# The W_d product of a decoder's first FFN as two float32r products of a split operand, and four instruction orders written anew

## The chip, the cores and the metric

The kernel runs on one core of one Trainium2 chip. The metric is the device time of one execution in microseconds (us); the smaller the better. Engines are named as in the profile: PE (TensorE matmuls), PEld (its weight loads), DVE (VectorE), ACT (ScalarE), POOL (GpSimd), SP (SyncE, which issues the DMAs).

## The reference

Input x is 16 sequences of 128 tokens with 256 features, and there is a context tensor of the same shape. Two decoder layers follow one another, each with post-norm residuals:

- layer 0: causal attention with 16 heads; a gated long convolution (per head an outer product of key and value, a causal convolution over the 128 positions, a product with the query); the first FFN;
- layer 1: a state-space mixer, a second long convolution, and a second FFN with a Hadamard transform.

The change is about the first FFN. For each token, x is normalised, scaled by 127 over its largest magnitude and rounded to an integer (`Q`). Then

```
g = Q @ sign(W_g).T      u = Q @ sign(W_u).T        (1024 columns each)
P = silu(inv * g) * (inv * u)                       (1024 columns, float32)
y = P @ sign(W_d).T                                 (256 columns)
x = norm(x + y)
```

so the last product multiplies full float32 numbers by a matrix that holds only -1, 0 and 1.

## The kernel before, in words

Everything stays in SBUF. A stage works item by item; an item is one sequence (128 tokens, one partition each), so each stage has 16 items, and the two long convolutions have 32 steps `mix(0)` to `mix(31)` each. Each stage is a Python function that returns small functions per engine (`f.down(n, k)`, `f.rstd(n)`, ...). The order in which an engine issues these calls is written out by hand in four functions, `tensor_order` (L1833), `scalar_order` (L1930), `vector_order` (L1999) and `gpsimd_order` (L2112); each engine runs its list strictly in order, and semaphores make a call wait for what it reads or overwrites. In the lists, `a` is attention, `m` the first convolution, `f` the first FFN, `x` the state-space mixer, `n` the second convolution, `g` the second FFN. Stages overlap only as far as the lists interleave them.

The first FFN (`ffn0`, L649 on) runs for item n:

- PE turns the convolution's result (L689), DVE adds x, takes the statistics and normalises (L804, L811, L819, L469), POOL computes 1/sqrt with two tiny instructions (L461, L463) and four more for the scale (L910 to L916, and L924); DVE finds the peak, the step and the integers (L831 to L855).
- PE turns Q (L698); `gate` and `up` multiply it by the signs of W_g and W_u, which are bf16, 512 columns at a time (L703).
- ACT takes the silu (L781), DVE multiplies (L863); the result `PM` is P with tokens on the partitions.
- `p_turn(n, k)` (L738) transposes half k of P, four blocks of 128x128, into a PSUM bank. For k = 1 that bank is also the one of `gate(n, 0)`.
- `keep_p(n, k)` (L788) copies that bank on ACT into `PMT`, 128x512 float32. There are two `PMT` buffers.
- `down(n, k)` (L750) makes four products of 256 columns; the eight of an item accumulate into one bank. The weights loaded into PE are blocks of P, the operand that streams through is sign(W_d), both float32.
- DVE adds x to the bank and normalises again (L871, L878, L880, L469), POOL gives 1/sqrt (L461, L463), PE turns the result for the next stage (L761), ACT keeps it (L794).

sign(W_d) is made by `sign0(2)` on ACT, in place (L524). Before the first FFN there is another piece of work that the orders place: the weights of the second FFN are loaded into staging tiles by SP (L502), once attention's last x is kept (`a.keep_x(15)`, L316, after PE's `a.x_turn(15)`, L264). ACT sums their magnitudes with `magnitude(0)` to `magnitude(2)` (L530), PE adds the sums over the partitions in `m.totals()` (L572), and its place in `tensor_order` is between two `mix` steps:

```
m.mix(16); a.x_turn(15)
m.mix(17); m.mix(18); m.mix(19); m.mix(20); m.mix(21); m.totals(); m.mix(22); ...
```

A `mix` step is three products of 512 float32 columns on PE (L594 to L596), two multiplications on POOL (L564), two on DVE (L608) and a sum on DVE (L619).

Of the kernel before, what the change touches and what calls it, by code (L numbers as in the profile page):

```python
# [9 lines left out]
BF16 = mybir.dt.bfloat16  # L10
ALU = mybir.AluOpType
# [3 lines left out]
P = 128  # L15
# [459 lines left out]
def mixer(ch, T, d, s, before, name, toep, skip, banks):  # L475
# [35 lines left out]
    def scalar(act):  # L511
# [9 lines left out]
        def sign0(k):  # L521
            dst, src = ((T["wgu0"][:, 1, :].rearrange("p (a w) -> p a w", a=2), T["wgu0_high"]), (T["wgu0"][:, 0, :], T["wgu0_low"]),
                        (T["wd0"][:, :, :], T["wd0"][:, :, :]))[k]
            nc.scalar.activation(dst, src, ACT.Sign).then_inc(s["signed"], 1)  # L524
# [123 lines left out]
def ffn0(ch, T, d, s, attended, mixed):  # L648
# [7 lines left out]
    PMT = two("pmt", [P, FC, S])  # L656
    ST, MV, VE, RS = two("st", [P, 6]), two("mv", [P, 2]), two("ve", [P, 1]), two("rs", [P, 1])
    ST3, MV3, VE3, RS3 = two("st3", [P, 6]), two("mv3", [P, 2]), two("ve3", [P, 1]), two("rs3", [P, 1])
    VA, VB, VC, RS2 = two("va", [P, 1]), two("vb", [P, 1]), two("vc", [P, 1]), two("rs2", [P, 1])
    MX, MS, SC, INV = two("mx", [P, 1]), two("ms", [P, 1], n=4), two("sc", [P, 1]), two("inv", [P, 1], n=4)  # L660
# [3 lines left out]
    X, XT, MIX, ident, identb, wgu, wd = (T[n] for n in ("X", "XT", "MIX", "ident", "identb", "wgu0", "wd0"))  # L664
# [12 lines left out]
    def tensor(pe):  # L677
# [28 lines left out]
        def gate(n, k):  # L706
# [7 lines left out]
            if k == 0:  # L714
                upto(pe, s["p1_kept"], n)
# [12 lines left out]
        def p_turn(n, k):  # L728
# [3 lines left out]
            upto(pe, s[f"p{k}_kept"], n)  # L732
# [33 lines left out]
    def scalar(act):  # L766
# [16 lines left out]
        def keep_p(n, k):  # L783
# [12 lines left out]
        return calls(keep_q=keep_q, silu=silu, keep_p=keep_p, keep_x=keep_x)  # L796

    def vector(dve):
# [67 lines left out]
        def add_down(n):  # L866
# [3 lines left out]
            dve.wait_ge(s["downed"], n + 1)  # L870
# [19 lines left out]
    def gpsimd(pool):  # L890
# [35 lines left out]
        return calls(rstd=rstd, rstd3=rstd3, rms=rms, step_back=step_back)  # L926
# [48 lines left out]
def state_space(ch, T, d, s, before):  # L975
# [345 lines left out]
    def gpsimd(pool):  # L1321
# [41 lines left out]
        def skip(n):  # L1363
# [3 lines left out]
            if n == 0:  # L1367
                pool.wait_ge(before["downed"], B)
# [962 lines left out]
```

## Time and profile before

| | us |
|---|---|
| median of 3 runs | 749.12 (746.75 to 749.25) |
| the profiled execution, its time | 746.65 |
| its span, first to last instruction | 744.0 |
| PE busy | 696.2 (94% of the span) |
| DVE busy | 610.1 (82%) |
| POOL busy | 538.3 (72%) |
| ACT busy | 412.4 (55%) |

"Busy" is the time in which at least one instruction of the engine ran. A matmul's recorded duration includes its way through the array and overlaps the next one, so what a matmul costs in a dense stretch is the distance from one start to the next, not the duration. PEclk is the granted TensorE clock as a share of full speed (1.00 is 2.4 GHz, 0.50 is 1.2 GHz).

### The profile page before, as it was taken

What the parts mean: (1) busy time and instruction counts of PE and PEld (TensorE: products, weight loads), DVE (VectorE), ACT (ScalarE), POOL (GpSimd) and SP (SyncE); (2) the same over time, 40 slices, a digit from 0 to 9 for tenths busy, and PEclk for the clock granted to TensorE, in tenths of its full rate; (3) what the DMA queues carried; (4) which work ended last, traced back from release to release, by engine and by line L of the source; (5) the groups of instructions that cost most, each with busy time, mean ns of one, the idle gap of its engine ahead of it and who ended that gap; (6) DMA issues with size and microseconds to landing.
All of it is one profiled execution on the core that took longest, in us unless ns stands there. A gap on an engine that the chain in (4) does not pass through costs nothing. (4 is left out here: it accounts for less than half of the span.)

```text
span 744.0 us, 13795 instructions
## 1 busy us (share of the span) xinstructions
PE 696.2 (94%) x4302; PEld 497.2 (67%) x4302; DVE 610.1 (82%) x1281; ACT 412.4 (55%) x660; POOL 538.3 (72%) x781
## 2 busy tenths in 40 slices
PE   6999999999989999999889989989999999999994
PEld 5788888754434677778667777755544457777783
DVE  4887888688979978665799899878999998877873
ACT  0665757710160744554598877872010348889784
POOL 2788798878857425530248668789898999999972
PEclk9999999999999999999999999999999999999997
DMA  8910000000300050000031121204000000000001
GB/s 282 365 52 2 2 2 3 1 1 0 141 29 1 0 217 1 1 2 1 29 103 72 44 71 34 80 1 131 1 0 1 0 2 1 15 16 15 9 22 44
DMA packets 12727, 33.39 MB, mean 45 GB/s; under 512 B 2672, under 2 KB 8048, under 8 KB 11376
## 3 DMA queue, kind: packets, MB, share of 16 engines
q1 hardware_dynamic: 12656, 32.52, 12.1%
q8 instruction: 36, 0.59, 0.3%
q14 instruction: 35, 0.29, 0.1%
HBM read 30.35 MB, written 2.16 MB: 44 GB/s over the span
## 5 line engine op out<-in xcount | busy, mean ns | idle before, releaser
L1053 PE MATMUL bank<-XT,win_late 128*128 128x256 f32 x320 | 81.3, 388 | 5.9 <-ACT ss_sz L1151 2.8
L564 POOL TENSOR_TENSOR m_kv<-CTXT 128x512 f32<-128x512 f32 x64 | 65.2, 1043 | 16.9 <-PE bank L596 16.9
L619 DVE TENSOR_REDUCE MIX<-m_pr 128x128 f32<-128x1024 f32 x64 | 77.0, 1210 | 0.3
L1238 DVE SCALAR_TENSOR_TENSOR ss_xc<-bank,cw_late,ss_xc 128x254 f32<-128x254 f32 x144 | 67.4, 477 | 4.9 <-ACT ss_xc L1142 1.4
L564 POOL TENSOR_TENSOR m_kv<-XT,CTXT 128x512 f32<-128x512 f32 x64 | 69.4, 1111 | 1.4 <-PE bank L596 1.1
L1053 PEld LDWEIGHTS bank<-XT,win_late 128*128 128x128 f32 x320 | 56.6, 190 | 17.6 <-DVE ss_xc L1238 5.6
L594 PE MATMUL bank<-m_kv,toep 128*128 128x512 f32 x128 | 66.1, 598 | 1.2 <-issue 1.2
L596 PE MATMUL bank<-m_kv,toep 128*128 128x512 f32 x128 | 66.3, 599 | 0.0
L595 PE MATMUL bank<-m_kv,toep 128*128 128x512 f32 x128 | 66.0, 597 | 0.0
L1530 PE MATMUL bank<-had_last,f_ht 128*128 128x256 f32 x256 | 60.2, 382 | 0.1
L750 PE MATMUL bank<-wd,f_pmt 128*128 128x256 f32 x256 | 59.7, 380 | 0.0
L461 POOL TENSOR_TENSOR f_ve<-f_mv,eps 128x1 f32<-128x1 f32 x48 | 9.4, 196 | 67.1 <-DVE f_mv L880 42.4
L1530 PEld LDWEIGHTS bank<-had_last,f_ht 128*128 128x128 f32 x256 | 47.3, 190 | 8.2 <-ACT f_ht L1593 0.9
L750 PEld LDWEIGHTS bank<-wd,f_pmt 128*128 128x128 f32 x256 | 47.3, 190 | 7.3 <-ACT f_pmt L788 0.5
L434 POOL TENSOR_TENSOR at_p<-at_p,at_mx 128x512 f32<-128x512 f32 x44 | 45.4, 1045 | 8.8 <-DVE at_mx L345 8.6
L280 ACT COPY at_pt<-bank 128x512 f32<-128x512 f32 x64 | 36.5, 590 | 20.4 <-PE bank L207 20.1
L596 PEld LDWEIGHTS bank<-m_kv,toep 128*128 128x128 f32 x128 | 24.6, 192 | 31.0 <-issue 31.0
L608 DVE TENSOR_TENSOR m_pr<-bank,XT 128x512 f32<-128x512 f32 x64 | 40.9, 682 | 5.3 <-PE bank L596 5.3
L595 PEld LDWEIGHTS bank<-m_kv,toep 128*128 128x128 f32 x128 | 24.3, 190 | 30.6 <-issue 30.6
L608 DVE TENSOR_TENSOR m_pr<-bank,CTXT 128x512 f32<-128x512 f32 x64 | 40.9, 682 | 2.6 <-PE bank L596 2.6
L160 PE MATMUL bank<-XT,at_wqk 128*128 128x128 f32 x256 | 34.6, 286 | 6.0 <-DMA at_hmask<-hmask_dram 5.6
L1142 ACT ACTIVATE ss_xc<-bank,cb_late,cw_late 128x256 f32<-128x256 f32 x48 | 26.9, 563 | 22.9 <-PE bank L1053 22.9
(247 smaller groups left out, 1884.8 us busy)
## 6 DMA issues: line engine op xcount, KB each, us to landing
MIX<-cum_rows SPq DMA_DIRECT2D x15, 512.0 KB, 3.4
toep<-toep_dram SPq DMA_DIRECT2D x2, 2048.0 KB, 12.4
X<-x_dram SPq DMA_DIRECT2D x1, 2048.0 KB, 12.5
CTXT<-ctxT_dram SPq DMA_DIRECT2D x1, 2048.0 KB, 17.6
out_dram<-f_o SPq DMA_DIRECT2D x16, 128.0 KB, 1.7
XT<-xT_dram SPq DMA_DIRECT2D x1, 1280.0 KB, 8.2
win_late<-win_dram SPq DMA_DIRECT2D x1, 1280.0 KB, 5.2
wgu<-wgu_dram SPq DMA_DIRECT2D x1, 1024.0 KB, 5.0
```

Source lines behind the costliest of these rows:

```text
L280: nc.scalar.copy(PTs[n % 2][:, 4 * t:4 * t + 4, :], bPT[t][:, :].rearrange("p (h s) -> p h s", h=4)).then_inc(pt_kept[t], 1)
L434: nc.gpsimd.tensor_tensor(v, v, MX[n % 2][:, 4 * t:4 * t + 4].unsqueeze(2).broadcast_to([P, 4, S]), ALU.subtract).then_inc(s["shifted"], 1)
L564: m = nc.gpsimd.tensor_tensor(KV[n % 3][:, c, :, :].rearrange("p (b j) i -> p b j i", b=HB), ki, vj, ALU.mult)
L594: nc.tensor.matmul(y[0][:, :], toep[:, a, 0:P], kv[0], start=True, stop=True)
L595: nc.tensor.matmul(y[1][:, :], toep[:, a, P:2 * P], kv[0], start=True, stop=False)
L596: nc.tensor.matmul(y[1][:, :], toep[:, a, 0:P], kv[1], start=False, stop=True).then_inc(s["conved"], 1)
L608: nc.vector.tensor_tensor(PR[n % 2][:, c, :, :].rearrange("p (b j) i -> p b j i", b=HB), bY[pair(n)][c][:, :].rearrange("p (b j i) -> p b ...
L619: nc.vector.tensor_reduce(head(MIX)[:, :, a, bass.ts(h, HB), :], PR[n % 2][:, :, :, :].rearrange("p c (b j) i -> p c b j i", b=HB), op=ALU ...
L750: m = nc.tensor.matmul(b6[:, 0:D], PMT[n % 2][:, r, :], wd[:, r, :], start=(r == 0), stop=(r == FC - 1))
L1053: m = nc.tensor.matmul(bX[(NU * g + n) % 3][:, 0:GS_], win[:, h, off:off + P], XT[:, h, bass.ts(g, GS_)], start=(h == 0), stop=(h == C - 1))
L1238: m = nc.vector.scalar_tensor_tensor(acc[:, :, sh:S], bank[:, :, 0:S - sh], cw[:, r, n:n + 1], acc[:, :, sh:S], ALU.mult, ALU.add)
L1530: m = nc.tensor.matmul(bV[k][:, bass.ts(r, 2 * P)], HT[:, 4 * k + 2 * r + i, :], had[:, i, :], start=(i == 0), stop=(i == 1))
```

## The change

P is split into a high and a low part, each float32r (a float32 word of which a product on PE takes fewer bits): PH is P rounded to float32r, PL = P - PH. Both are multiplied by sign(W_d), now also float32r, into the same bank. Per half of an item ACT copies the bank twice (`round_p` into PH, `keep_p` into PMT), POOL subtracts (`rest_p`), and PE makes four products with PH and four with PL. PMT has one buffer where it had two; PH and PL have one each. The semaphores count accordingly (`p_kept` 2 per half, `downed` 4 per item). Many one-column tiles of the stage become columns of one tile. All four order lists are new, for all stages. In the new `tensor_order`, among much else, `a.x_turn(15)` stands after `m.mix(13)` and `m.totals()` after `m.mix(20)`, and the first `a.value(0)` stands after the first three `a.qk`; in `scalar_order`, `m.sign0(2)` stands after the magnitudes.

```
-    PMT = two("pmt", [P, FC, S])
+    PMT, = two("pmt", [P, FC, S], n=1)
+    PH, PL = (two(n, [P, FC, S], F32R, n=1)[0] for n in ("ph", "pl"))
...
             if k == 0:
-                upto(pe, s["p1_kept"], n)
+                upto(pe, s["p1_kept"], 2 * n)              # gate(n, 0)
...
-            upto(pe, s[f"p{k}_kept"], n)
+            upto(pe, s[f"p{k}_kept"], 2 * n)               # p_turn(n, k)
...
-        def down(n, k):
+        def down(n, low, k):
...
-            pe.wait_ge(s[f"p{k}_kept"], n + 1)
-            if k == 0:
+            if low:
+                pe.wait_ge(s["p_rest"], 2 * n + k + 1)
+            else:
+                pe.wait_ge(s[f"p{k}_kept"], 2 * n + 1)
+            if not low and k == 0:
                 upto(pe, s["down_free"], n)
...
+            part = PL if low else PH
             for r in range(4 * k, 4 * k + 4):
-                m = nc.tensor.matmul(b6[:, 0:D], PMT[n % 2][:, r, :], wd[:, r, :], start=(r == 0), stop=(r == FC - 1))
-            if k:
-                m.then_inc(s["downed"], 1)
+                m = nc.tensor.matmul(b6[:, 0:D], part[:, r, :], wd[:, r, :], start=(r == 0 and not low), stop=(r == FC - 1 and low == 1))
+            m.then_inc(s["downed"], 1)
...
         def keep_p(n, k):
             act.wait_ge(s[f"p{k}_turned"], n + 1)
-            upto(act, s["downed"], n - 1)
-            nc.scalar.copy(PMT[n % 2][:, 4 * k:4 * k + 4, :], bP[k] ...).then_inc(s[f"p{k}_kept"], 1)
+            upto(act, s["p_rest"], 2 * n - 1 + k if n else 0)
+            nc.scalar.copy(PMT[:, 4 * k:4 * k + 4, :], bP[k] ...).then_inc(s[f"p{k}_kept"], 1)
+
+        def round_p(n, k):
+            act.wait_ge(s[f"p{k}_turned"], n + 1)
+            upto(act, s["p_rest"], 2 * n - 1 + k if n else 0)
+            upto(act, s["downed"], 4 * n - 3 + k)
+            nc.scalar.copy(PH[:, 4 * k:4 * k + 4, :], bP[k] ...).then_inc(s[f"p{k}_kept"], 1)
...
-            dve.wait_ge(s["downed"], n + 1)
+            dve.wait_ge(s["downed"], 4 * n + 4)            # add_down(n)
...
+        def rest_p(n, k):
+            pool.wait_ge(s[f"p{k}_kept"], 2 * n + 2)
+            upto(pool, s["downed"], 4 * n - 1 + k)
+            quarter = slice(4 * k, 4 * k + 4)
+            nc.gpsimd.tensor_tensor(PL[:, quarter, :], PMT[:, quarter, :], PH[:, quarter, :].bitcast(F32), ALU.subtract).then_inc(s["p_rest"], 1)
...
+        with ExitStack() as ch.scope:
+            whole(("wd0", [P, FC, D], F32))
+        ch.scope = ch.whole
+        whole(("wd0_sign", [P, FC, D], F32R), ...
```

A steady stretch of the new `tensor_order` and of the new `gpsimd_order`:

```
f.p_turn(7, 1); f.up(8, 1); f.down(6, 1, 0); f.down(6, 1, 1); f.x_turn(3); f.p_turn(7, 0); f.q_turn(9); f.gate(8, 0); f.up(8, 0); f.down(7, 0, 0);
f.mix_turn(13); f.down(7, 0, 1); f.down(7, 1, 0); f.q_turn(10); f.gate(9, 1); f.up(9, 1); f.p_turn(8, 1); f.down(7, 1, 1); f.p_turn(8, 0); ...
f.rms(9); f.step_back(8); f.step_back(9); f.rstd(10); f.rms(10); f.rest_p(6, 0); f.rest_p(6, 1); f.rstd(11); f.step_back(10); f.rms(11); ...
```

## Rows read from the trace of the kernel before

**Rows 1.** Busy by stretch: us, PE, PEld, DVE, ACT, POOL (instructions), PEclk, DMA, GB/s

```profile
0.00:187.00 187.00, 176.47 (x1616) 135.08 (x1617) 146.77 (x279) 93.90 (x161) 145.23 (x181) 1.00 0.19 71
187.00:249.50 62.50, 56.31 (x158) 25.72 (x157) 56.59 (x96) 21.50 (x22) 41.31 (x61) 0.97 0.13 51
249.50:353.00 103.50, 103.50 (x583) 81.91 (x582) 74.70 (x217) 51.55 (x95) 41.47 (x126) 1.00 0.11 40
353.00:470.00 117.00, 105.83 (x652) 84.84 (x651) 104.27 (x226) 92.79 (x140) 72.24 (x80) 1.00 0.17 60
470.00:600.00 130.00, 123.53 (x474) 68.78 (x473) 118.76 (x211) 41.21 (x67) 119.72 (x147) 1.00 0.08 28
600.00:744.00 144.00, 130.58 (x826) 100.91 (x824) 109.03 (x257) 111.49 (x178) 118.31 (x190) 0.96 0.05 16
```

**Rows 2.** Groups by line, stretch 249.5 to 353: busy, mean ns, idle before

```profile
L750 PE MATMUL bank<-wd,f_pmt 128*128 128x256 f32 x256 | 59.7, 380 | 0.0
L863 DVE SCALAR_TENSOR_TENSOR f_pm<-bank,f_inv,f_sl 128x512 f32<-128x512 f32 x30 | 22.2, 745 | 8.5 <-ACT f_sl L781 6.3 <-PE bank L703 1.9
L781 ACT ACTIVATE f_sl<-bank,f_inv 128x512 f32<-128x512 f32 x30 | 20.2, 694 | 7.0 <-PE bank L703 6.9
L788 ACT COPY f_pmt<-bank 128x512 f32<-128x512 f32 x30 | 17.1, 588 | 27.1 <-PE bank L738 26.9
L463 POOL TENSOR_TENSOR f_rs<-f_ve,mhalf 128x1 f32<-128x1 f32 x28 | 16.0, 571 | 2.2
L871 DVE TENSOR_TENSOR f_y<-bank,X 128x256 f32<-128x256 f32 x16 | 6.8, 422 | 13.3 <-PE bank L750 13.2
L461 POOL TENSOR_TENSOR f_ve<-f_mv,eps 128x1 f32<-128x1 f32 x27 | 5.2, 191 | 51.5 <-DVE f_mv L880 37.1 <-DVE f_mv L819 14.4
```

**Rows 3.** Instructions in time, PE, inside the first FFN: start, us, count

```profile
286.54 0.60 PE L738 MATMUL bank<-ident,f_pm 128*128 128x128 f32 x4
...
287.09 1.89 PE L703 MATMUL bank<-wgu,f_qt 128*128 128x512 bf16 x8
...
289.04 1.89 PE L750 MATMUL bank<-wd,f_pmt 128*128 128x256 f32 x8
```

**Rows 4.** POOL's 128x512 subtraction in attention: duration ns min/median/max, starts

```profile
L434 POOL TENSOR_TENSOR at_p<-at_p,at_mx x44: 1037/1042/1140, 16.1 to 142.5; 128x512 f32<-128x512 f32 x44
```

**Rows 5.** DVE's normalisation (L469): in the first FFN, and from 470 to 600

```profile
L469 DVE TENSOR_SCALAR X<-f_y,f_mv,f_rs x28: 382/405/570, 249.8 to 350.7; 128x256 f32<-128x256 f32 x28
...
L469 DVE TENSOR_SCALAR X<-ss_y,ss_mv,ss_rs x9: 383/1115/1285, 480.3 to 547.4; 128x256 f32<-128x256 f32 x9
```

**Rows 6.** Instructions in time, DVE beside POOL

```profile
233.73 2.08 POOL L564 TENSOR_TENSOR m_kv<-CTXT 128x512 f32<-128x512 f32 x2
233.76 1.16 DVE L848 TENSOR_SCALAR f_z<-X,f_sc 128x256 f32<-128x256 f32 x1
234.84 1.12 DVE L469 TENSOR_SCALAR X<-f_y,f_mv,f_rs 128x256 f32<-128x256 f32 x1
```

**Rows 7.** Instructions in time, from attention's last turned x to the totals

```profile
187.90 0.38 PE L264 MATMUL bank<-ident,X 128*128 128x128 f32 x2
...
196.06 0.38 PE L264 MATMUL bank<-ident,X 128*128 128x128 f32 x2
...
196.94 0.33 SPq L502 DMA_DIRECT2D wg_staged<-wg_dram  x1
...
206.62 1.91 ACT L530 ACTIVATE m_junk<-wg_staged 128x2048 bf16<-128x2048 f32 x1 [9.77 <-DMA wd_raw_staged<-wd_dram]
...
212.84 0.35 PE L572 MATMUL bank<-m_wpart,m_ones 128*128 128x3 f32 x2 [3.52 <-ACT m_junk L530]
```

**Rows 8.** Busy by stretch, as in the first group: behind that wait

```profile
212.00:220.00 8.00, 7.16 (x16) 3.45 (x17) 4.04 (x7) 6.68 (x5) 2.04 (x2) 0.79 0.00 0
```

**Rows 9.** Instructions in time, the first products of attention

```profile
9.21 1.17 PE L172 MATMUL bank<-at_wv,XT 128*128 128x256 f32 x4
...
10.37 2.02 PE L160 MATMUL bank<-XT,at_wqk 128*128 128x128 f32 x16
```

More of the change, by code:

```diff
@@ L10 @@
 BF16 = mybir.dt.bfloat16
+F32R = mybir.dt.float32r
 ALU = mybir.AluOpType
@@ new lines, in tensor_order @@
+    f.down(2, 1, 0); f.p_turn(3, 1); f.mix_turn(8); f.down(2, 1, 1); f.q_turn(4); f.q_turn(5); f.gate(4, 1); f.gate(4, 0); f.mix_turn(9); f.up(4, 1)
+    f.gate(5, 1); f.p_turn(3, 0); f.up(4, 0); f.down(3, 0, 0); f.down(3, 0, 1); f.p_turn(4, 1); f.down(3, 1, 0); f.up(5, 1); f.down(3, 1, 1)
+    f.x_turn(0); f.gate(5, 0); f.p_turn(4, 0); f.up(5, 0); f.mix_turn(10); f.down(4, 0, 0); f.q_turn(6); f.down(4, 0, 1); f.gate(6, 1)
+    f.down(4, 1, 0); f.down(4, 1, 1); f.up(6, 1); f.p_turn(5, 1); f.p_turn(5, 0); f.q_turn(7); f.up(6, 0); f.down(5, 0, 0); f.x_turn(1)
@@ new lines, in tensor_order @@
+    f.down(5, 0, 1); f.gate(6, 0); f.down(5, 1, 0); f.gate(7, 1); f.down(5, 1, 1); f.mix_turn(11); f.p_turn(6, 1); f.q_turn(8); f.up(7, 1)
+    f.p_turn(6, 0); f.x_turn(2); f.gate(7, 0); f.up(7, 0); f.gate(8, 1); f.mix_turn(12); f.down(6, 0, 0); f.down(6, 0, 1); f.p_turn(7, 1); f.up(8, 1)
+    f.down(6, 1, 0); f.down(6, 1, 1); f.x_turn(3); f.p_turn(7, 0); f.q_turn(9); f.gate(8, 0); f.up(8, 0); f.down(7, 0, 0); f.mix_turn(13)
+    f.down(7, 0, 1); f.down(7, 1, 0); f.q_turn(10); f.gate(9, 1); f.up(9, 1); f.p_turn(8, 1); f.down(7, 1, 1); f.p_turn(8, 0); f.up(9, 0)
@@ new lines, in tensor_order @@
+    f.gate(9, 0); f.x_turn(4); f.gate(10, 1); f.down(8, 0, 0); f.down(8, 0, 1); f.down(8, 1, 0); f.down(8, 1, 1); f.mix_turn(14); f.up(10, 0)
+    f.p_turn(9, 0); f.q_turn(11); f.p_turn(9, 1); f.up(10, 1); f.down(9, 0, 0); f.q_turn(12); f.gate(11, 1); f.x_turn(5); f.gate(10, 0)
+    f.down(9, 0, 1); f.down(9, 1, 0); f.down(9, 1, 1); f.p_turn(10, 1); f.up(11, 1); f.p_turn(10, 0); f.up(11, 0); f.gate(11, 0); f.mix_turn(15)
+    f.down(10, 0, 0); f.q_turn(13); f.gate(12, 1); f.down(10, 0, 1); f.p_turn(11, 1); f.x_turn(6); f.up(12, 1); f.down(10, 1, 0); f.down(10, 1, 1)
@@ new lines, in tensor_order @@
+    f.p_turn(11, 0); f.gate(12, 0); f.up(12, 0); f.x_turn(7); f.gate(13, 1); f.q_turn(14); f.down(11, 0, 0); f.p_turn(12, 1); f.down(11, 0, 1)
+    f.p_turn(12, 0); f.down(11, 1, 0); f.down(11, 1, 1); f.up(13, 1); f.gate(13, 0); f.up(13, 0); f.down(12, 0, 0); f.p_turn(13, 1); f.gate(14, 1)
+    f.x_turn(8); f.p_turn(13, 0); f.q_turn(15); f.up(14, 1); f.down(12, 0, 1); f.down(12, 1, 0); f.down(12, 1, 1); f.up(14, 0); f.x_turn(9)
+    f.gate(14, 0); f.down(13, 0, 0); f.gate(15, 1); f.p_turn(14, 1); f.down(13, 0, 1); f.down(13, 1, 0); f.down(13, 1, 1); f.p_turn(14, 0)
@@ new lines, in tensor_order @@
+    f.up(15, 1); f.gate(15, 0); x.unit(0, 0); f.up(15, 0); f.x_turn(10); f.down(14, 0, 0); f.p_turn(15, 1); f.p_turn(15, 0); f.x_turn(11)
+    f.down(14, 0, 1); f.down(14, 1, 0); f.down(14, 1, 1); x.unit(0, 1); x.unit(0, 2); f.down(15, 0, 0); f.x_turn(12); f.down(15, 0, 1)
+    f.down(15, 1, 0); f.down(15, 1, 1); x.unit(0, 3); f.x_turn(13); x.unit(0, 4); f.x_turn(14); x.unit(0, 5); f.x_turn(15); x.dt_product()
+    x.dt_turn(); x.unit(0, 6); x.unit(0, 7); x.unit(0, 8); x.unit(0, 9); x.unit(1, 0); x.unit(1, 1); x.x_back(0); x.unit(1, 2); x.sums(); x.x_back(1)
@@ L2181, in program, with whole @@
     with ch.whole:
-        T = {n: ch.sb(n, s, t) for n, s, t in (
+        T = {}
+        def whole(*names):
+            T.update((n, ch.sb(n, shape, t)) for n, shape, t in names)
+        whole(
             ("X", [P, B, D], F32), ("XT", [P, C, NT], F32), ("CTXT", [P, C, NT], F32), ("MIX", [P, C, NT], F32),
```

648 lines of the change are left out of this document (322 added, 326 removed).

## The prediction, made before the changed kernel was run

> **What bounds the kernel now.** I read the busy times by stretch first. The first FFN, from the first W_d product to the last (249.5 to 353), keeps PE busy for 103.5 of 103.5 us, while DVE has 74.7, ACT 51.6 and POOL 41.5 [rows 1]. So in this stage PE alone sets the end, and a us less of PE work is worth a us until the next engine is full. No other stage looks like this: from 353 to 600 PE and DVE share the work at about 90% and 95%, with POOL as high from 470 on [rows 1].
>
> Next the groups by line say what PE does there. The W_d product is 59.7 of the 103.5 us, in 256 records [rows 2]. The code has 16 items times 8 products, so a float32 product is two records. In time, eight such records take 1.89 us; with the last one's 0.38 taken off, that is seven starts, one every 0.216 us, for 256 columns each [rows 3]. Eight bf16 records of 512 columns take the same 1.89 us [rows 3]: bf16 streams twice as many columns in the same time, in one record per product. A float32 transpose is one record of 128 columns every 0.109 us ((0.60 - 0.27)/3) [rows 3]. So a product of 256 columns costs 0.432 us in float32, and would cost 0.108 at bf16's rate and 0.216 at the transpose's.
>
> Who is late behind PE: DVE waits 13.2 us for the W_d product (L871), ACT 26.9 us for the turned P, and POOL 51.5 us for statistics [rows 2]. All three have room; the question is how much of it the change uses.
>
> Last, PE stands idle for 3.52 us at 209 to 213, waiting for ACT's sums of the staged weights before `m.totals()` [rows 7], and in the 8 us behind it the granted clock is 0.79 on average, that is 1.7 us' worth of columns lost, at the 1.2 GHz level [rows 8]. That is 5.2 us in one place.
>
> **The change part by part.**
>
> *Products.* Removed: 256 records of 0.216, 55.3 us. Added: 16 items times 16 products of 256 columns, 256 products. No row shows float32r. From below it can't beat bf16's column rate, 0.108; from above it is a float32 product, 0.432; between them lies 0.216, one record at the transpose's rate. I take 0.108, 27.6 us: the operand is of reduced precision by its type and the float32 product's two records point to a product put together from parts, of which this needs one. Also, weights of 128 float32 columns have been loaded every 0.109 us beside the transposes, so the loads do not hold it back further. PE's work in the stretch is then 103.5 - 55.3 + 27.6 = 75.8 us.
>
> The Trainium skill bears on the size: "FP8 and Floating Point Precision", TensorE Precision Notes, states that true FP32 takes four passes through the array, and that reduced-precision FP32 reads the word and truncates it. The trace agrees with the four passes (0.432 is four times 0.108). By this rule the new product is one pass, and the sum is as above; no run here shows it yet.
>
> *ACT.* 32 more copies of a 128x512 bank. The copy is 0.588 [rows 2]; rounding on the way out may cost nothing more or up to the silu of that shape, 0.694. I take 0.588: 18.8 us, ACT 70.4. Hidden, as ACT idles for 27 us before these copies [rows 2]; but they lengthen the way from P to product, and the bank that `gate(n, 0)` needs is held for two copies and not for one.
>
> *POOL.* 32 subtractions of 128x512 from SBUF. The subtraction of that shape in attention takes 1.04 us at the median, 1.04 to 1.14 at the ends [rows 4]: 33.3 us. POOL comes to 74.8, and with the gaps between its small dependent instructions (2.2 us at L463 alone) to about 78. Behind a waiting `rest_p` are queued the next items' rstd and rms, on which DVE's normalisation waits; and the low products wait for it.
>
> *DVE.* Nothing is added to its list, but it meets POOL. In the first FFN before, POOL has no large instruction and L469 takes 0.405 at the median; from 470 to 600, where POOL is 92% busy, it takes 1.115 at the median [rows 1, 5]. One case in time: L848 and L469 start inside two POOL multiplications and last 1.16 and 1.12, until these end [rows 6]. In the changed stage large POOL instructions fill 33.3 of some 93 us, 36% of the time, and a DVE instruction that falls into one waits half of it, 0.52. Three such SBUF-only float32 instructions per item (both norms and the lift) make 48 x 0.36 x 0.52 = 9 us. From below 0; from above each of the 48 loses 0.7 as at 470 to 600, 34 us. I take 9: DVE is then at about 84 us, the fullest engine.
>
> The Trainium skill has this as a rule: "SBUF — State Buffer", Who interferes with whom, says that DVE's single-source instructions in a 2-port mode and GpSimd share one port pair, and whoever comes second waits for the whole instruction. The trace agrees in kind with the 1.16 us instead of 0.35 to 0.41.
>
> *The stage's length.* With DVE 84, POOL 78, PE 76 and ACT 70 four engines are nearly full. In the two stages before that look so, the fullest engine has 95% (470 to 600) and 90% (353 to 470) [rows 1]. Here the in-order chains are longer, so I take 90%: 84/0.9 = 93. The stage loses 10.5 us. The ends: none of it, and 103.5 - 84 = 19.5 with DVE never idle (25.5 if DVE and POOL never met and POOL's 78 decided, 27.7 if PE alone did).
>
> *The wait before `m.totals()`.* Before, `a.x_turn(15)` starts at 196.06; the DMA is issued 0.88 later, ACT starts its sums at 206.62 and PE gets them at 212.84 [rows 7]: 16.8 us from the turn. Between the turn and the totals PE had five `mix` steps. Three such steps and two turned x (`a.x_turn(13)` to `a.x_turn(15)`) took 196.06 - 187.90 = 8.2 us, so a step is about 2.6, five are 13.1, and 3.5 were missing. Now seven steps lie between (14 to 20), 18.2 us, against the same 16.8. The wait goes, with 1.4 us to spare, and with it the half clock, which came right behind PE's idle time. In exchange the turn comes three steps earlier and can itself wait for the norm of item 15; DVE's list has that norm right behind `times_q(12)`, one step ahead of it. I take the whole 5.2 us; the end from below is 0 (the wait moves to the turn). DVE is idle for 5.9 of the 62.5 us around it [rows 1], so it allows 5.2, barely.
>
> *Moved calls elsewhere.* `a.value(0)` no longer fills PE's time between the first qk and the second: 1.17 us of work that stood in an otherwise idle gap of 9.4 to 10.37 [rows 9], so up to 1.2 us more. The other moves keep all instructions, their counts and shapes. PE's idle time outside the two places is about 10 us in the first 187, 11 and 6 in 353 to 600, 13 in the last 144 [rows 1]; a new order can win or lose a part of it. I take 0, with 4 us either way. `sign0(2)` moves behind the sums; it is needed only at the first W_d product. The tiles' new places cost nothing.
>
> **Sum.** The profiled execution took 746.65 (744.0 of span and 2.65 around it). 746.65 - 10.5 - 5.2 = 731. The median of the runs lies 2.5 above the profiled one, so 733.4; I say 733.
>
> **The rivals.**
>
> 1. *POOL's list holds up the low products.* `rest_p` stands behind rms chains that wait for DVE, DVE waits for the low products, and the stage ends at 101, with only the totals' wait won: 749.1 - 2.5 - 5.2 = 741. For it: POOL is at 78 with two-way dependence on DVE. Against: it had 62 us free.
> 2. *float32r runs at the transpose's rate*, 0.216 per product: PE stays at 103.5, the longer chain adds some 2 us, the totals give 5: 746. For it: the float32 transpose is one record and yet slow. Against: the four-to-one above.
> 3. *The single buffers put the items in a row* (slower). PMT, PH and PL exist once, so if the lists let item n+1 begin only when item n's low part is subtracted, one item takes two multiplications 1.49, turns 0.60, four copies 2.35, two subtractions 2.08, the last products 0.43 and the silu 0.69: 7.6 us. The pace before is 103.5/16 = 6.5; above it the change loses: 16 x 1.1 - 5.2 gives 762. Against: the new list has `p_turn(7, 1)` before `down(6, 1, 1)`, so halves of two items overlap.
> 4. *float32r costs what float32 does*, 0.432: 55 us more PE work, 799.
> 5. *The moved calls cost more than the rest gives*: about 750. The lists are different everywhere, and 35 us of PE idle time is where a wrong guess of a DMA or a meeting of DVE and POOL would show.
>
> **How the numbers follow.** The forecast has 0.66, the rivals in order 0.14, 0.06, 0.07, 0.03 and 0.04. A measurement of this kernel tells about 0.5% from no change, 3.7 us: faster is below 745.4, slower above 752.9. The forecast lies wholly below; rival 1 mostly (0.12), rival 2 with a third. Faster 0.80, within 0.5% 0.07, slower 0.13. The range for 8 in 10: below, the stage at its 84 us bound with the totals' gain is 749.1 - 19.5 - 5.2 = 724, and 2 more for the moves, 722; above, rivals 1 and 2 are in and 3, 4 and part of 5 out: 748.
>
> **What would show it.** Right: 256 records at the new product with starts 0.108 apart, about 28 us in all; the stage from first to last W_d product 90 to 96 us with DVE the fullest engine; L469 at a mean of 0.5 to 0.7 there, not 0.41; no wait before the totals and PEclk 1.00 behind it. Wrong: starts 0.216 apart or two records per product; PE idle before the new `down` on POOL's `rest_p` for more than 10 us in all; PE still waiting 3 us or more for ACT's sums or for the turn of item 15; or another stage more than 4 us longer than before.

## The result, and the profile after

The changed kernel takes 726.57 us (median of 4 runs, 723.57 to 727.97), the kernel before 747.93 beside it: a ratio of 0.971, 95% interval 0.967 to 0.976. The forecast was 733, its range 722 to 748. The profiled execution took 727.97, of which the span is 726.0; the span before was 744.0.

First the busy times by stretch. Columns: stretch, its length, then PE, PEld, DVE, ACT, POOL, PEclk, DMA share, GB/s.

```profile
0.00:184.80 184.80, 177.73 (x1624) 137.57 (x1625) 147.73 (x283) 94.28 (x163) 145.73 (x183) 1.00 0.19 72
184.80:243.30 58.50, 54.24 (x149) 24.32 (x149) 55.63 (x93) 19.41 (x21) 40.55 (x60) 0.97 0.14 54
243.30:347.00 103.70, 88.39 (x569) 66.27 (x577) 80.81 (x210) 68.39 (x127) 79.53 (x154) 0.97 0.11 40
347.00:482.40 135.40, 125.64 (x802) 103.57 (x801) 126.42 (x275) 112.85 (x170) 100.55 (x106) 1.00 0.17 60
482.40:590.00 107.60, 106.37 (x348) 54.25 (x349) 102.71 (x175) 24.09 (x42) 102.83 (x131) 1.00 0.08 23
590.00:726.00 136.00, 123.98 (x796) 98.55 (x806) 103.14 (x251) 107.70 (x172) 111.87 (x184) 0.96 0.05 17
```

The cuts are attention's last turned x, the first and the last W_d product, the last input product of the state-space stage (`x.unit`), the last `mix` step of the second convolution, and the end of the span. The first cut can't be compared with before, since that turn stands three `mix` steps earlier in the new list; the others can. They are not all those of [rows 1], so here are the same ones, from the first W_d product on, in the trace of before:

```profile
249.70:351.70 102.00, 102.00 (x575) 80.61 (x574) 73.34 (x213) 51.34 (x95) 41.41 (x125) 1.00 0.11 41
351.70:493.40 141.70, 127.44 (x785) 102.58 (x785) 125.81 (x272) 110.20 (x166) 91.85 (x101) 1.00 0.16 57
493.40:607.40 114.00, 110.50 (x373) 56.25 (x372) 105.78 (x180) 26.96 (x46) 107.02 (x133) 1.00 0.07 22
607.40:744.00 136.60, 123.31 (x800) 96.80 (x798) 101.63 (x245) 108.34 (x172) 111.40 (x183) 0.96 0.05 17
```

The first W_d product starts at 249.7 before and at 243.3 after, the last one at 351.7 and 347.0. So of the 18.0 us of span, 6.4 are won ahead of the first W_d product; the first FFN, which the change is about, is 1.7 us longer (102.0 to 103.7); and 13.3 are won behind it, where only the order of calls is new: 6.3 in the state-space stage, 6.4 in the second convolution, 0.6 in the rest. The 1.7 are no more than one execution differs from another: experiment 4 below has the same lists up to the end of the first FFN, the same waits, and a stage of 102.0. Where the two differ is the granted clock in the ten us behind PE's longest wait there, first in the changed kernel, then in experiment 4:

```profile
260.00:270.00 10.00, 8.98 (x44) 6.12 (x45) 7.42 (x21) 5.80 (x10) 3.41 (x7) 0.66 0.00 1
260.00:270.00 10.00, 8.73 (x51) 6.02 (x50) 8.55 (x23) 6.67 (x11) 5.06 (x9) 0.83 0.00 1
```

0.83 - 0.66 over ten us is 1.7 us' worth of columns, the whole difference. So the stage is as long as before, and lengths of stages with idle times of PE are compared below to within about 2 us.

Inside the stage PE fell from full to 88.4 us of 103.7, and no other engine took its place: DVE has 80.8, POOL 79.5, ACT 68.4. The groups by line in this stretch, against [rows 2] (busy us, mean ns, idle time before them and what ended it):

```profile
L945 POOL TENSOR_TENSOR f_pl<-f_pmt,f_ph 128x512 fp32r<-128x512 f32 x32 | 40.9, 1299 | 10.3 <-ACT f_pmt L793 8.2 <-PE bank L756 1.9
L756 PE MATMUL bank<-wd_sign,f_ph 128*128 128x256 f32 x128 | 22.7, 306 | 1.7 <-ACT f_ph L801 1.7
L756 PE MATMUL bank<-wd_sign,f_pl 128*128 128x256 f32 x128 | 22.2, 302 | 9.3 <-POOL f_pl L945 9.0
L793 ACT COPY f_pmt<-bank 128x512 f32<-128x512 f32 x31 | 18.5, 604 | 0.0
L470 DVE TENSOR_SCALAR X<-f_y,f_mv,f_columns 128x256 f32<-128x256 f32 x27 | 18.2, 680 | 7.6 <-POOL f_columns L464 7.5
L801 ACT CAST f_ph<-bank 128x512 fp32r<-128x512 f32 x30 | 17.6, 592 | 22.3 <-PE bank L740 13.0 <-POOL f_pl L945 8.8 <-PE bank L756 0.3
L884 DVE TENSOR_TENSOR f_y<-bank,X 128x256 f32<-128x256 f32 x15 | 6.3, 419 | 8.3 <-PE bank L756 8.3
```

`rest_p` on POOL (L945) holds up PE (9.0 us) and ACT's next `round_p` (8.8), and itself waits for ACT (8.2). DVE's normalisation waits 7.5 us for POOL's 1/sqrt, where it waited 2.1 in the stage of before; that `rest_p` in POOL's list is the reason is likely and not shown. The 256 old records, two per float32 product, are gone; there are now 128 with PH and 128 with PL, one per product. Their spacing is read in time:

```profile
335.03 0.72 PE L756 MATMUL bank<-wd_sign,f_ph 128*128 128x256 f32 x4
335.59 1.11 PE L756 MATMUL bank<-wd_sign,f_pl 128*128 128x256 f32 x8
336.54 0.60 PE L740 MATMUL bank<-ident,f_pm 128*128 128x128 f32 x4
```

Eight products of 256 columns are started in 336.54 - 335.59 = 0.95 us, 0.119 each, against 0.432 for a float32 product worked out from [rows 3]. The group of four with PH ahead of them is started in 0.56 us, 0.14 each, so a short group costs a little more per product. (The busy time of a short group is longer than its starts, since the last record's own length is in it; that is why 256 products sum to 44.9 us here.)

The wait ahead of `m.totals()` [rows 7] is gone:

```profile
202.05 1.02 PE L597 MATMUL bank<-m_kv,toep 128*128 128x512 f32 x2
202.91 0.28 PE L573 MATMUL bank<-m_wpart,m_ones 128*128 128x3 f32 x2
...
232.90 1.02 PE L597 MATMUL bank<-m_kv,toep 128*128 128x512 f32 x2
237.12 3.19 PE L705 MATMUL bank<-wgu,f_qt 128*128 128x512 bf16 x7 [3.20 <-DVE m_pr L609]
```

The totals start at 202.91 and no longer at 212.84, 9.9 us earlier; 2.6 of these are the one `mix` step by which they moved forward in the list. The last `mix` step of the first convolution shows what was won, 8.9 us (before, then after):

```profile
240.12 1.08 PE L594 MATMUL bank<-m_kv,toep 128*128 128x512 f32 x2
231.18 1.02 PE L595 MATMUL bank<-m_kv,toep 128*128 128x512 f32 x2
```

6.4 are left at the first W_d product. PE now waits 3.2 us for DVE's last multiplication of the first convolution (1.6 before), at a lower clock, and from 202.9 to 243.3 DVE is busy for 37.98 of 40.40 us, the fullest engine. The half clock of [rows 8] is gone from its place (PEclk 1.00 from 210 to 230), but there is half clock behind PE's new idle times: PEclk is 0.86 over 230 to 240, and 0.66 over 260 to 270, behind a wait of 2.10 us at 259.77 for POOL's f_pl.

### The profile page after: what moved, and what is told of

Same layout as the page of the kernel before. It is cut to its first block and busy times, and to the rows that moved or that the text cites. A ratio compares the mean times of both kernels' runs of the same rounds, so it can differ in the third digit from the quotient of the medians.

```text
span 726.0 us, 13897 instructions
## 1 busy us (share of the span) xinstructions
PE 676.3 (93%) x4278; PEld 484.5 (67%) x4302; DVE 616.4 (85%) x1281; ACT 426.7 (59%) x692; POOL 581.1 (80%) x813
## 3 DMA queue, kind: packets, MB, share of 16 engines
q1 hardware_dynamic: 12656, 32.52, 12.4%
## 5 line engine op out<-in xcount | busy, mean ns | idle before, releaser
L1074 PE MATMUL bank<-XT,win_late 128*128 128x256 f32 x320 | 79.3, 385 | 2.2 <-DVE ss_xc L1259 1.7
L565 POOL TENSOR_TENSOR m_kv<-XT,CTXT 128x512 f32<-128x512 f32 x64 | 67.2, 1078 | 2.3 <-PE bank L597 2.3
L435 POOL TENSOR_TENSOR at_p<-at_p,at_mx 128x512 f32<-128x512 f32 x44 | 45.0, 1042 | 13.3 <-DVE at_mx L346 12.8
L945 POOL TENSOR_TENSOR f_pl<-f_pmt,f_ph 128x512 fp32r<-128x512 f32 x32 | 40.9, 1299 | 10.3 <-ACT f_pmt L793 8.2
L705 PE MATMUL bank<-wgu,f_qt 128*128 128x512 bf16 x118 | 36.6, 410 | 4.7 <-DVE m_pr L609 3.2
L161 PEld LDWEIGHTS bank<-XT,at_wqk 128*128 128x128 f32 x256 | 33.1, 209 | 8.3 <-DMA at_hmask<-hmask_dram 5.7
L288 ACT ACTIVATE at_p<-at_p 128x1024 f32<-128x1024 f32 x22 | 23.4, 1064 | 20.5 <-POOL at_p L435 20.5
## 6 DMA issues: line engine op xcount, KB each, us to landing
X<-x_dram SPq DMA_DIRECT2D x1, 2048.0 KB, 12.4
```

The lines of the kernel that those rows point to most:

```text
L161: m = nc.tensor.matmul(b0[:, bass.ts(g, S)], wqk[:, c, bass.ts(g, P)], XT[:, c, tok(n)], start=(c == 0), stop=(c == C - 1))
L435: nc.gpsimd.tensor_tensor(v, v, MX[n % 2][:, 4 * t:4 * t + 4].unsqueeze(2).broadcast_to([P, 4, S]), ALU.subtract).then_inc(s["shifted"], 1)
L565: m = nc.gpsimd.tensor_tensor(KV[n % 3][:, c, :, :].rearrange("p (b j) i -> p b j i", b=HB), ki, vj, ALU.mult)
L945: nc.gpsimd.tensor_tensor(PL[:, quarter, :], PMT[:, quarter, :], PH[:, quarter, :].bitcast(F32), ALU.subtract).then_inc(s["p_rest"], 1)
L1074: m = nc.tensor.matmul(bX[(NU * g + n) % 3][:, 0:GS_], win[:, h, off:off + P], XT[:, h, bass.ts(g, GS_)], start=(h == 0), stop=(h == C - 1))
```

## The experiments

Two questions: is the gain from the split or from the orders, and why did the first FFN not get shorter? "Stage" below is the time from the first W_d product's start to the last one's, "tail" that from there to the end of the span. In the cuts of code "..." marks what is left out; line breaks inside the order lists are not kept.

**1. The changed orders with the old product.** All lists in their new order, `round_p`, `rest_p` and the low `down` left out, `down(n, k)` and the stage's tiles as before.

```diff
-f.down(6, 0, 0); f.down(6, 0, 1); f.p_turn(7, 1); f.up(8, 1); f.down(6, 1, 0); f.down(6, 1, 1)
+f.down(6, 0); f.down(6, 1); f.p_turn(7, 1); f.up(8, 1)
```

> The new orders with the old W_d product: float32, two P buffers, one copy per half on ACT, nothing on POOL. Theory A (the split itself earns nothing; PE's saving in the first FFN was handed over to the subtraction on POOL, and the 21 us come from the new orders, above all behind the first FFN): 723 to 731 us, first to last W_d product 98 to 106 us. Theory B (the split earns its 10 to 14 us inside the new orders, which count on a PE that has room): the stage takes 112 to 118 us, as PE's work there is 88.7 + 27.7 us, and the whole 735 to 741 us.

731.18 us, ratio 0.978 (0.976 to 0.981). Three quarters of the gain come from the order of calls alone. The time lies 0.2 us above theory A's range and 4 below B's, the stage between the two: the split earns something inside the new orders, but less than half of what B had. The stage takes 109.3 us in this order, the tail 376.1:

```profile
244.50:353.80 109.30, 104.73 (x577) 81.21 (x576) 71.97 (x213) 53.98 (x95) 41.49 (x125) 1.00 0.10 38
```

**2. The split in the orders of before.** Lists of before; `round_p` ahead of each `keep_p`, the low products behind the high ones of their item, `rest_p` added to POOL's list as late as the other lists allow.

```diff
-f.down(6, 0); f.p_turn(7, 1); f.down(6, 1); f.p_turn(7, 0)
+f.down(6, 0, 0); f.p_turn(7, 1); f.down(6, 0, 1); f.down(6, 1, 0); f.down(6, 1, 1); f.p_turn(7, 0)
```

> The split in the old orders: each keep_p has its round_p ahead of it, each pair of down calls is followed by the two low ones, and POOL's subtractions stand as late as the other lists allow. Theory A: the stage from first to last W_d product is not shorter than the 102 us of before, 102 to 115, and the whole 747 to 760 us. Theory B: 90 to 97 us, the whole 735 to 743 us.

773.78 us, ratio 1.036 (1.031 to 1.040): slower than both theories had it. The stage takes 125.3 us. The waits in it (engine, tile and line waited for; us in total, times, longest):

```profile
ACT f_ph L801 <- PE bank L740: 33.2, 16, 8.2
PEld bank L756 <- POOL f_pl L945: 24.0, 19, 5.9
PE bank L756 <- POOL f_pl L945: 19.8, 15, 5.7
```

`p_turn(7, 0)` stands behind `down(6, 1, 1)`, which waits for `rest_p(6, 1)`: PE stands still for POOL and ACT for PE. The items come in a row, as rival 3 described; the same split takes 103.7 us in the changed kernel's lists, so it is the list that makes the row. The granted clock is 0.92 over this stage, some 10 of its 125.3 us' worth of columns, behind these waits. This is one placement of the new calls in the old lists; a better one was not tried.

**3. The new order only behind the first FFN**, with the kernel before up to each engine's last call of the first FFN.

```diff
...
-x.unit(2, 5); x.out_product(0); x.x_back(3); x.unit(2, 6); x.unit(2, 7); x.square_sum(1); x.unit(2, 8); x.scan(2)
+x.c_times_b(3); x.unit(2, 6); x.square_sum(0); x.x_back(3); x.unit(2, 7); x.unit(2, 8); x.scan(2)
...
```

> The kernel before, with the new orders only behind the last call of the first FFN (state space, second convolution, second FFN); everything up to there, the float32 W_d product too, as before. Theory A: what the new kernel gains behind its first FFN (13 of 18 us of span) comes from these orders: 733 to 738 us. Theory B, here: it comes from the state in which the first FFN hands over (DVE and POOL less behind, other work already done): 745 to 751 us.

730.74 us, ratio 0.978 (0.975 to 0.981). With nothing of the split and nothing ahead of it, the late lists earn 15.6 us (746.31 for the kernel before, beside it), more than theory A's range; B is out. The tail falls from 392.3 to 376.1:

```profile
354.00:488.00 134.00, 125.72 (x802) 103.71 (x801) 124.99 (x271) 112.79 (x170) 98.41 (x102) 1.00 0.18 60
488.00:595.50 107.50, 106.39 (x350) 54.19 (x348) 102.58 (x175) 24.08 (x42) 102.67 (x131) 1.00 0.08 23
595.50:730.10 134.60, 123.58 (x808) 98.03 (x806) 102.79 (x251) 107.70 (x172) 111.51 (x184) 0.98 0.05 17
```

**4. The reverse**: the changed kernel with the late lists of before.

```diff
...
-x.c_times_b(3); x.unit(2, 6); x.square_sum(0); x.x_back(3); x.unit(2, 7); x.unit(2, 8); x.scan(2)
+x.unit(2, 5); x.out_product(0); x.x_back(3); x.unit(2, 6); x.unit(2, 7); x.square_sum(1); x.unit(2, 8); x.scan(2)
...
```

> The changed kernel with its own first FFN and all that is ahead of it, but behind each engine's last call of the first FFN the calls stand in the order of the kernel before. Theory A (the late orders are worth the same some 15 us wherever they stand, since they shorten the stretch from the last product with W_d to the end, 392.3 us before and 376.1 us with the old FFN and the new late orders): the stretch goes back from 379.0 to 391-395 us and the kernel takes 738-743 us, nearly the whole of the gain undone. Theory B (the late part only picks up what the first FFN hands it late, so that its order matters little behind the faster early part): 729-734 us.

740.07 us, ratio 0.990 (0.987 to 0.993); the stage is 102.0, the tail 393.7. Theory A holds: the late lists are worth 13.5 us here and 15.6 behind the old FFN, so they depend little on what hands the work to them.

**5. Only the state-space calls (`x.`) in the new order among themselves**, the calls of the second convolution and the second FFN as before.

```diff
...
-x.unit(3, 0); x.unit(3, 1); x.unit(3, 2); x.scan(3); x.out_product(1); x.unit(3, 3)
+x.unit(3, 0); x.unit(3, 1); x.c_times_b(4); x.x_back(4); x.unit(3, 2); x.square_sum(1); x.out_product(1)
...
```

> The kernel before, with only the calls of the state-space stage among themselves in the changed kernel's order (the slots of all other calls on each engine kept). Theory A (the gain of the late orders is made in the state-space stage, and the second convolution's start only inherits it): the stretch from the last W_d product to the last state-space unit goes from 141.7 to 133-135 us as with all late orders, and the kernel takes 732-737 us. Theory B (the gain is spread: each stage's hand-over to the next one earns a part, 7.7 us by the last state-space unit, 6.5 more by the end of the second convolution, 2.0 behind it): 739-744 us.

753.14 us, ratio 1.008 (1.006 to 1.010). Both theories fall, though A's stretch comes out as it said:

```profile
353.50:487.50 134.00, 125.69 (x802) 103.69 (x801) 125.00 (x271) 112.76 (x170) 98.45 (x102) 1.00 0.17 60
487.50:615.00 127.50, 113.48 (x357) 57.94 (x356) 105.95 (x181) 24.34 (x42) 105.69 (x132) 0.95 0.06 20
```

The state-space stage gets its 134.0 us as in experiment 3, and the stretch behind it takes 127.5 in the place of 107.5, where the kernel before has 114.0. PE's longest waits there, of which experiment 3 has 0.2 us in that stretch:

```profile
PE bank L1092 <- POOL ss_sq L1361: 6.6, 2, 5.6
PE bank L1083 <- DVE MIX L1252: 4.7, 1, 4.7
```

Here the state-space stage's new list was worth its gain only with the lists of the next stages that were made with it. The `x.` calls also kept the places of the old ones among the other calls, so this is not quite the new list by itself.

**6. Without the low part**: no `keep_p`, no `rest_p`, no low `down` (P rounded to float32r alone).

```diff
-f.down(6, 0, 0); f.down(6, 0, 1); f.p_turn(7, 1); f.up(8, 1); f.down(6, 1, 0); f.down(6, 1, 1)
+f.down(6, 0, 0); f.down(6, 0, 1); f.p_turn(7, 1); f.up(8, 1)
...
-f.round_p(6, 1); f.keep_p(6, 1)
+f.round_p(6, 1)
```

> The changed kernel without its low part: the products with PH alone, no second copy on ACT and no subtraction on POOL, so P enters the W_d product at reduced precision. Theory A (the stage of 104 us is set by the way over POOL: 32 subtractions of 1.3 us, and PE's and ACT's waits for them): the stage falls to 82 to 90 us, the whole to 706 to 714 us. Rival (DVE or the orders set the stage and the low part is beside it): the stage stays at 97 to 104 us and the whole at 720 to 727 us.

700.29 us, ratio 0.938 (0.934 to 0.942), stage:

```profile
242.80:318.90 76.10, 68.44 (x449) 48.33 (x448) 68.17 (x208) 53.53 (x96) 41.61 (x125) 1.00 0.15 54
```

The low part costs the stage 103.7 - 76.1 = 27.6 us, more than the 25 us that the change saves in products, and more than theory A had asked (its stage was 82 to 90).

**7. The low products, but without making PL**: as 6, and the low `down` reads PH a second time.

```diff
-                pe.wait_ge(s["p_rest"], 2 * n + k + 1)
+                pe.wait_ge(s[f"p{k}_kept"], n + 1)
...
-            part = PL if low else PH
+            part = PH
```

> The changed kernel without ScalarE's float32 copy and GpSimd's subtraction, but with all 16 products of an item: the low ones read PH a second time in the place of PL. It costs TensorE what the change costs it and nothing else; high_only, without these products, had a stage of 76.1 us and 700.3 us. Theory A (the low products cost TensorE their own spacing, 128 x 0.117 = 15 us, and the rest of the change's 27.6 us in the stage comes from making PL): stage 88-93 us, kernel 711-716 us. Theory B (making PL costs nothing of its own; it is TensorE's list with four more steps an item that sets the stage): stage 99-104 us, kernel 723-728 us.

707.35 us, ratio 0.946 (0.945 to 0.948). The stage:

```profile
242.50:327.90 85.40, 80.70 (x577) 64.47 (x576) 69.43 (x208) 53.34 (x96) 41.20 (x123) 1.00 0.13 48
```

Of the 27.6 us, PE's 128 products cost 9.3 and making PL (copy, subtraction, hand-over) 18.3. Theory A, by more than it had asked.

**8 and 9. The subtraction on DVE**, from the PSUM bank: of half 1 (8), of both halves (9). The float32 copy of that half and its subtraction on POOL go.

```diff
+        def rest_v(n, k):
...
+            dve.wait_ge(s[f"p{k}_kept"], 2 * n + 1)
+            upto(dve, s["downed"], 4 * n - 1 + k)
...
+            nc.vector.tensor_tensor(PL[:, quarter, :], bP[k][:, :].rearrange("p (r s) -> p r s", r=4), PH[:, quarter, :].bitcast(F32),
+                                    ALU.subtract).then_inc(s[f"p{k}_kept"], 1)
...
 f.multiply(6, 0); f.add_x(11); f.lift(9); f.aggregate(10)
+f.rest_v(6, 1)
```

> The changed kernel with the low part of half 1 made by VectorE straight from the PSUM bank (bank minus PH, 128x512, to PL), without ScalarE's float32 copy of that half and without GpSimd's subtraction of it; half 0 as it was. Theory A (the first FFN waits for GpSimd's two subtractions of 1.26-1.45 us in a row, behind which TensorE and ScalarE's next copies stand): GpSimd's busy time in the stage falls from 80 to some 59 us, ScalarE's from 68 to 59, VectorE's rises from 81 to 85-90, TensorE's idle time ahead of the low products goes, the stage from the first to the last W_d product takes 94-99 us instead of 103.7, and the kernel 717-723 us. Theory B (VectorE's chain of the item is what sets the stage, GpSimd's wait only stands in front of it): VectorE's 16 more instructions of 0.7 us come on top, the stage takes 105-115 us and the kernel 728-738 us.

> As the last one, but both halves' low parts are made by VectorE from the PSUM banks; neither the float32 copies on ScalarE nor GpSimd's subtractions are left. Theory A (GpSimd's path was the limit, and VectorE gets back the 5-9 us that its normalisations lose beside GpSimd): VectorE has 81 + 22 - 8 = 95 us of work in the stage and is its fullest engine, level with TensorE's 89-92; the stage takes 96-101 us and the kernel 719-725 us, 1-3 us more than with one half. Theory B (VectorE's chain sets the stage): 32 more instructions of 0.7 us in its order, the stage takes 115-125 us and the kernel 738-748 us.

728.22 us (0.972 to 0.977 of before) and 732.35 us (0.977 to 0.982), stages of 104.2 and 108.9. Experiment 8 is theory B's but for its stage, just under B's 105; in 9 the time and the stage lie between the two theories. POOL's busy time in the stage fell to 60.5 and 41.4, DVE's rose to 83.5 and 90.2, and the stage got no shorter: POOL's load was not the limit. In 8, PE's waits changed their name:

```profile
PE bank L705 <- DVE f_pl L904: 9.7, 11, 2.5
PE bank L758 <- DVE f_y L887: 3.1, 3, 1.4
PE bank L758 <- POOL f_pl L957: 1.5, 3, 0.7
```

The gate of half 0 shares its bank with the turned P of half 1, and that bank is now free only when DVE has subtracted. With both halves on DVE the same wait is 11.1 us, though L470 no longer meets a POOL subtraction (mean 398 ns in the place of 680); PEclk is 0.95 there, so some 2 of its 108.9 us more than in the changed kernel are the clock's.

**10. The low products two calls later in PE's list.**

```diff
-f.up(8, 1); f.down(6, 1, 0); f.down(6, 1, 1); f.x_turn(3); f.p_turn(7, 0); f.q_turn(9)
+f.up(8, 1); f.x_turn(3); f.p_turn(7, 0); f.down(6, 1, 0); f.down(6, 1, 1); f.q_turn(9)
```

> The changed kernel with each of the low products' calls moved two calls later in TensorE's list (not past the next product call), so that TensorE finds other work while GpSimd subtracts. Theory A (the 8-9 us that TensorE stands idle before low products are lost to the stage since it is next in its list): its idle time there falls under 4 us, stage 97-101 us, kernel 719-724 us. Theory B (the wait is a symptom: what the low products give back late is then missed by VectorE's addition of the item, which waits for them 7.6 us already): stage 103-107 us, kernel 726-731 us.

730.35 us, ratio 0.978 (0.976 to 0.979), stage 106.8. Of PE's 9.0 us of waiting for f_pl 0.8 are left, but PE is idle for 19.7 us of the stage in all (15.3 in the changed kernel), now for DVE's and ACT's results; DVE's wait for the finished product doubled, from 8.3 us in the changed kernel to

```profile
DVE f_y L884 <- PE bank L756: 15.7, 10, 3.1
```

Theory B: to let PE do other work first did not give the 9 us back.

**11. The split on half 0 only**; half 1 by one copy and four float32 products.

```diff
-                m = nc.tensor.matmul(b6[:, 0:D], part[:, r, :], wd[:, r, :], start=(r == 0 and not low), stop=(r == FC - 1 and low == 1))
+                m = nc.tensor.matmul(b6[:, 0:D], PMT[:, r, :] if k else part[:, r, :], wd[:, r, :].bitcast(F32) if k else wd[:, r, :], start=(r == 0 and not low), stop=(r == 3 and low == 1))
```

> The changed kernel with the split on half 0 only: half 1 goes by one float32 copy and four float32 products, as in the kernel before. GpSimd has 16 subtractions less (-20.8 us), ScalarE 16 copies less (-9.4 us), TensorE 64 float32 products at some 0.43 us in the place of 128 at 0.117 us (+12.5 us, to some 101 us of work in the stage's 103.7). Theory A (making PL in time is the limit, so half of it is worth more than the slower products): stage 97-101 us, kernel 720-724 us. Theory B (TensorE is as good as full again): stage 104-109 us, kernel 727-732 us.

717.20 us, ratio 0.960 (0.958 to 0.962): 1.3% under the changed kernel, with intervals that do not touch, and better than theory A asked. The stage:

```profile
241.20:337.70 96.50, 92.77 (x577) 73.53 (x576) 74.60 (x212) 61.30 (x112) 61.15 (x140) 1.00 0.11 43
```

PE is 96% busy, never waits more than 1.3 us in all for any one producer, and the clock stays at 1.00 in this stage (0.97 in the changed kernel). It is the fastest of the kernels here that leave no part of P out.

**12. As 11, with the one low part made by DVE** from its bank, which no gate shares.

```diff
-            nc.gpsimd.tensor_tensor(PL[:, quarter, :], PMT[:, quarter, :], PH[:, quarter, :].bitcast(F32), ALU.subtract).then_inc(s["p_rest"], 1)
+            nc.vector.tensor_tensor(PL[:, 0:4, :], bP[0][:, :].rearrange("p (r s) -> p r s", r=4), PH[:, 0:4, :].bitcast(F32),
+                                    ALU.subtract).then_inc(s["p0_kept"], 1)
```

> half_split (717.2 us, stage 96.5) with the one low part that is left, that of half 0, made by VectorE from its PSUM bank, so that neither the float32 copy of that half nor any subtraction on GpSimd is left. The bank of half 0 is, unlike that of half 1, not also the bank of a gate. Theory A (rest_half_dve and rest_all_dve gained nothing because TensorE's gates then waited some 10 us for VectorE to give the bank free; without that, work taken from GpSimd and ScalarE is worth time): stage 90-95 us, kernel 711-716 us. Theory B (VectorE's place in the loop is as dear as GpSimd's: another 16 x 0.69 = 11 us in its list come on top): stage 97-102 us, kernel 718-723 us.

727.59 us, ratio 0.973 (0.971 to 0.975), stage 105.0: worse than both theories' ranges. No gate waits for DVE now, but DVE waits for ACT in its own list, and PE for DVE's addition (L886) 5.0 us:

```profile
DVE f_pl L902 <- ACT f_ph L803: 12.7, 12, 2.3
```

In this and in 8 and 9 I placed the calls by one rule (three calls behind the item's second multiplication, in 9 the other half's two calls later); what a better place would give was not tried.

## Why the prediction was right in its number and wrong in its main reason

- **The products: right.** One record each, 0.119 us apart where 0.108 was forecast, a float32 product 0.432. 256 of them are 30 us, not 27.6, and a little more in short groups. The Trainium skill's "FP8 and Floating Point Precision", TensorE Precision Notes, has true FP32 in four passes. The trace agrees roughly: the float32 product takes 3.6 times as long as the new one.
- **ACT: right.** The rounding copy takes 0.592 us, the plain one 0.604 in this stage; 68.4 us against 70.4.
- **POOL: the load right, its parts off.** 79.5 against 78 us; but one subtraction takes 1.30 and not the 1.04 of [rows 4], 40.9 us in all for 33.3, while the gaps added to the forecast are not busy time.
- **DVE: the load right.** 80.8 against 84. L470's mean is 0.680 (0.5 to 0.7 forecast). The quantisation to bf16, which the forecast left out, meets POOL too: up to 1.398 us, where it never took over 0.296 in this stage before. By the means of before and after, norms, lift and quantisation lose 10.5 us (9 forecast); about 3 us of other work that stood in the stage before now stands outside it. But DVE is not the fullest engine, as forecast: PE is.
- **The stage's length, 93 us: this is the step that failed.** The four loads were all within 13 us of the forecast, PE's 88.4 us the farthest off, and the stage still did not shrink (103.7; 102.0 in experiment 4). "Here the in-order chains are longer, so I take 90%" was the error: the fullest engine reached 85%. Experiments 6 and 7 measure what was missed: without making PL the same PE list takes 85.4 us, and making PL adds 18.3 (about 3 of them are PEclk 0.97 for 1.00, behind PE's waits). Experiments 8 to 10 point to a loop and not one engine: taking the subtraction off POOL, or PE off its wait, renames the wait (a gate's bank, DVE's addition) and leaves 104 to 109. Making less of PL helps: experiment 11, with half of it gone and 12.4 us more of products (64 at 0.432 for 128 at 0.119), takes 96.5. That takes 18 us off POOL, 7 off ACT and 6 off DVE as well as steps off the chain, so the two are not separated there. Nor is it tested what the single buffers add: ACT's 8.8 us of waiting for `rest_p` are, by the semaphores, waits for the one PH and PMT, and no run has two of PMT, PH or PL. Rival 1 had the place and nearly the price (101 us); it was given 0.14. Its mark, PE idle for over 10 us on `rest_p`, was missed narrowly, at 9.0. Its reason is not borne out: `rest_p` itself waits for ACT's copy (8.2 us), and experiment 10, which takes PE off that wait, gains nothing.
- **What the split is worth, then:** in the new lists 731.2 - 726.6 = 4.6 us, by a stage of 103.7 against 109.3. The two ratios' intervals touch, at 0.976, while no run of the one is as fast as the slowest of the other. That stage of the old product in the new list is longer than the 102.0 that it takes in its own list. So against the kernel before, the stage earns nothing.
- **The wait ahead of the totals: right where it stood.** Both the wait and the half clock behind it are gone: `mix(17)` starts 3.7 us earlier than before (attention's part), `mix(22)` 7.1 (the wait), `mix(23)` 9.1 (the half clock and what stood behind it), and the last one 8.9. The forecast let all of the 5.2 us reach the end, but 2.5 us are lost again between the last `mix` step and the first W_d product, in PE's wait for DVE and the lower clock there. So 6.4 are left, of which some 3.5 are attention's. No run undoes these early orders by themselves, and the first W_d product starts anywhere from 241.2 to 244.6 in the runs that share them.
- **The moved calls, "0, with 4 us either way": the term that was mis-sized.** They gave 3.5 us in attention (its first turned x starts at 81.7 and not at 85.2), where PE's idle time from 20 to 160 went from 4.1 us to 0.4, and 13.3 behind the first FFN (13.5 and 15.6 us of the kernels' times in experiments 4 and 3). The 31 us of PE idle time behind 353 stood in [rows 1]; I had read them as something that a new order can as well lengthen as shorten.

The total was right by luck, because two misses cancelled: 10.5 us forecast for the stage and not there, about 13 behind it not forecast and there. Rival 5, which had the moved calls cost more than the rest gives, had the wrong sign.

Left open: which of the late calls carry the gain (the four engines' late lists were only exchanged together, and experiment 5 shows that the stages' lists belong together); what part of the 18.3 us is the chain, the single buffers, and the clock; and why the tail is 376.1 us in experiments 1 and 3 and 377 to 380 in the others with the same late lists (379.0 in the changed kernel).

## What to carry to other kernels

When a saturated engine is relieved by handing work to others, add up the chain of one item (wait, copy, subtract, product, bank free) beside the loads: here, with every engine at 65 to 85% and single buffers, the loads alone did not set the pace, and moving a step to a freer engine only renamed the wait. Splitting only as much as empties the full engine (half, here) can beat splitting all. When a diff reorders calls throughout, give the reordering a term of its own, sized by the idle time of the busiest engine, and undo it by itself first; it was worth more here than the arithmetic in its title.

## What the hardware showed that was not expected

- POOL's 128x512 subtraction into PL, which is float32r, takes longer than attention's into float32, in the same execution of the changed kernel (duration ns min/median/max, first and last start):

```profile
L435 POOL TENSOR_TENSOR at_p<-at_p,at_mx x44: 1039/1042/1046, 17.9 to 135.8; 128x512 f32<-128x512 f32 x44
...
L945 POOL TENSOR_TENSOR f_pl<-f_pmt,f_ph x32: 1259/1285/1449, 244.5 to 344.4; 128x512 fp32r<-128x512 f32 x32
```

 The second also has another kind of operands (two full tiles); which of the two costs the 0.24 us was not separated. On ACT writing float32r costs nothing more (0.592 against 0.604), and DVE makes the same subtraction from PSUM in 0.684 (experiment 9).
- DVE's TENSOR_SCALAR instructions on one SBUF tile are held by a POOL subtraction even when they write bf16:

```profile
258.37 2.64 POOL L945 TENSOR_TENSOR f_pl<-f_pmt,f_ph 128x512 fp32r<-128x512 f32 x2
258.51 0.42 DVE L824 BATCH_NORM_STATS2 f_st<-f_y 128x6 f32<-128x256 f32 x1
258.85 1.02 DVE L868 TENSOR_SCALAR f_q<-f_z 128x256 bf16<-128x256 f32 x1
...
259.79 1.37 DVE L470 TENSOR_SCALAR X<-f_y,f_mv,f_columns 128x256 f32<-128x256 f32 x1
```

 The quantisation takes 1.02 us where its median is 0.286, the normalisation 1.37 where it is 0.413; the statistics, inside the same pair of subtractions, keep their 0.42. "SBUF — State Buffer", Who interferes with whom, in the Trainium skill has DVE instructions in a 2-port mode wait so, `tensor_scalar` among them. The trace agrees in kind; it does not show the mode.
- A float32r product of 256 columns every 0.119 us goes on while each weight load is recorded with 0.188 us: the recorded length of a load is not the distance that it sets.
